# First attention: four tasks of its software pipeline change their slots, and the square of q and k moves behind an exponential

## The reference

```python
qkv = x @ Wqkv.T + bqkv                    # x: layer-normed, (16, 256, 128)
q, k, v = (qkv[:, :, 0], qkv[:, :, 1], qkv[:, :, 2])   # 16 heads of 8 channels
q = rms_norm(q, qn_w)                      # q / sqrt(mean(q*q) + 1e-6) * w, for each head
k = rms_norm(k, kn_w)
scores = jnp.einsum('bhsd,bhtd->bhst', q, k) * scale
attn = jax.nn.softmax(scores, axis=-1)
out = jnp.einsum('bhst,bhtd->bhsd', attn, v)
return out.reshape(B, S, D) @ Wproj.T + bproj          # added to x
```

## Time and profile before

| | before |
|---|---|
| median of 3 runs | 1019.81 us (1018.68 to 1025.88) |
| the profiled execution | 1023.82 us, span 1022.0 us |
| mean granted clock of TensorE | 0.965 |
| busy: PE / PEld / DVE / ACT / POOL | 86% / 61% / 71% / 57% / 51% |
| exponentials of attention a (L414) | 128, 1024 ns each, 33.1 us idle in front of them |
| values of attention a (L315) | 1024 matmuls, 72.0 us busy |

### The profile page before, as it was taken

The page is one execution under the profiler, slowest core; times in us unless marked ns, Lnnn a source line. Parts: engine busy times, 40 slices in busy tenths (PEclk is TensorE's granted clock), DMA queues, the critical chain, the costliest instruction groups (busy, mean ns, idle before and its releaser), DMA issues.

```text
span 1022.0 us, 22245 instructions
## 1 busy us (share of the span) xinstructions
PE 883.0 (86%) x7264; PEld 625.6 (61%) x7264; DVE 728.8 (71%) x1970; ACT 579.1 (57%) x905; POOL 523.8 (51%) x606
## 2 busy tenths in 40 slices
PE   0589899987899999998788888888888789999998
PEld 0245555544588787886655555555554578878887
DVE  4357777766677777775657989898885477767765
ACT  1177777766544344443358888888886444344443
POOL 2556666656155545552425565666644364455441
PEclk9999999999799999998859999999997899999999
DMA  8000000000000000000000000000000000000000
GB/s 227 0 2 2 0 0 0 0 1 2 2 1 1 1 1 1 0 1 1 0 1 2 2 1 0 0 0 0 1 2 1 1 10 2 13 11 10 10 11 22
DMA packets 14591, 8.70 MB, mean 9 GB/s; under 512 B 1600, under 2 KB 14144, under 8 KB 14528
## 3 DMA queue, kind: packets, MB, share of 16 engines
q1 hardware_dynamic: 12944, 7.28, 2.5%
q10 hardware_dynamic: 1584, 0.62, 0.2%
HBM read 5.80 MB, written 2.10 MB: 8 GB/s over the span
## 4 chain that ended last, share of the span: by engine, by line
PE 21%; issue 13%; DVE 11%; POOL 7%; ACT 2%; DVEq 0%; POOLq 0%; ACTq 0%
DVE s_qs L1028 6%; PE psum L759 5%; PE psum L727 4%; POOL f_xe_lo L1374 3%; POOL f_p L1384 3%; PE psum L1267 2%; PE psum L709 2%; PE psum L1229 1%; PE psum L814 1%; DVE f_xe L1411 1%; PE psum L825 1%; PE psum L1231 1%; PE psum L1230 1%; PE psum L744 1%; ACT f_xe_hi L1343 1%
## 5 line engine op out<-in xcount | busy, mean ns | idle before, releaser
L1343 ACT ACTIVATE f_xe_hi<-f_xe 128x512 fp32r<-128x512 f32 x128 | 80.9, 632 | 202.8 <-DVE f_xe L1411 202.8
L1028 DVE TENSOR_REDUCE s_qs<-psum 128x4 fp32r<-128x1024 f32 x128 | 156.5, 1222 | 42.9 <-PE psum L744 42.2
L1374 POOL TENSOR_TENSOR f_xe_lo<-f_xe,f_xe_hi 128x512 fp32r<-128x512 f32 x64 | 83.7, 1308 | 192.7 <-ACT f_xe_hi L1343 192.7
L1267 PEld LDWEIGHTS psum<-w,f_h 128*128 128x128 f32 x1152 | 148.5, 192 | 8.8
L1267 PE MATMUL psum<-w,f_h 128*128 128x128 f32 x1152 | 153.8, 277 | 0.0
L414 ACT ACTIVATE s_probs<-psum 128x1024 f32<-128x1024 f32 x128 | 125.6, 1024 | 33.1 <-PE psum L301 32.9
L895 ACT ACTIVATE s_probs<-psum 128x1024 f32<-128x1024 f32 x128 | 131.2, 1025 | 19.2 <-PE psum L727 17.6
L1427 DVE TENSOR_TENSOR f_h<-psum,f_g 128x512 f32<-128x512 f32 x144 | 99.2, 689 | 49.2 <-ACT f_g L1328 33.9
L1229 PE MATMUL psum<-f_xe_hi,w_hi 128*128 128x512 f32 x288 | 127.6, 443 | 7.7 <-POOL f_xe_lo L1374 7.0
L1231 PE MATMUL psum<-f_xe_lo,w_hi 128*128 128x512 f32 x288 | 114.4, 397 | 0.0
L1230 PE MATMUL psum<-f_xe_hi,w_lo 128*128 128x512 f32 x288 | 113.8, 395 | 0.0
(11 more groups left out here) (179 smaller groups left out, 1757.1 us busy)
## 6 DMA issues: line engine op xcount, KB each, us to landing
x<-in_x SPq DMA_DIRECT2D x4, 512.0 KB, 9.5
out<-x SPq DMA_DIRECT2D x8, 256.0 KB, 2.3
w<-in_w SPq DMA_DIRECT2D x3, 512.0 KB, 6.7
select_raw<-in_select SPq DMA_DIRECT2D x1, 512.0 KB, 4.9
rope_cos<-in_rope_cos SPq DMA_DIRECT2D x1, 256.0 KB, 3.6
rope_sin<-in_rope_sin SPq DMA_DIRECT2D x1, 256.0 KB, 4.5
wqkv_a<-in_Wqkv_aT ACTq DMA_DIRECT2D x1, 192.0 KB, 6.0
bqkv<-in_bqkv ACTq DMA_DIRECT2D x1, 192.0 KB, 6.8
```

Source lines behind the costliest of these rows:

```text
L1028: dve.tensor_reduce(o[:, r:r + 2, 2 * p:2 * p + 2, 24:25].bitcast(F32R), M.rearrange("p (r j s) -> p r j s", r=2, j=2), AX.X, ALU.max, neg ...
L1267: ins = pe.matmul(Y[k % 2][:, t * P:(t + 1) * P], g.f_h[:, q, t * P:(t + 1) * P], g.w2[:, e, :], start=(e == 0 and t == 0), stop=(e == NE ...
L1374: pool.tensor_tensor(xe_lo[:, ring(e), :], src, xe_hi[:, ring(e), :], ALU.subtract).then_inc(xe_lo_pool.sem, 1)
```

## The change

Four tasks change their slots, and the key copy gets an entry of its own. In `AT_A`: normalise 8 to 10; x_turn 10 to 15; square, v copy 6 to 7; k_turn(1) 11 to 12; o_turn(1) 6 to 8, tokens(1) 7 to 8. The key copies stood in the slots of the k_turns, 7 and 11, and stand now in 7 and 13 (`kt_keep`). On ScalarE the code of the square moves ahead of that of the key copies, so that in slot 7 the order is exps(7), square, key copy.

```diff
--- before.py
+++ after.py
@@ -212,14 +212,15 @@
 
 
 STAGE_A = {"norm": 3, "xb": 2, "xt": 3, "qkv": 2, "square": 2, "sums": 2, "newton": 2, "rms": 2, "split": 1, "lo": 1,
-           "v": 1, "kt": 1, "qp": 1, "xt_keep": 3, "otr": -1, "atr": -1, "at_keep": -1, "pj": -1, "tokens": -1,
+           "v": 1, "kt": 1, "kt_keep": 1, "qp": 1, "xt_keep": 3, "otr": -1, "atr": -1, "at_keep": -1, "pj": -1, "tokens": -1,
            "residual": -1, "rstd": -1}
 
 
 AT_A = {
-    "pv": 5, "norm": (8,), "xb": (13,), "xt": (10,), "xt_keep": (15,), "qkv": (2, 4), "square": (6,), "sums": (7,),
-    "newton": (7,), "rms": (12,), "split": (2, 1), "lo": (3, 2), "v": (6,), "kt": (7, 11), "qp": (9, 14),
-    "otr": (3, 6), "tokens": (3, 7), "atr": (10,), "at_keep": (11,), "pj": (14,), "residual": (15,), "rstd": (15,),
+    "pv": 5, "norm": (10,), "xb": (13,), "xt": (15,), "xt_keep": (15,), "qkv": (2, 4), "square": (7,), "sums": (7,),
+    "newton": (7,), "rms": (12,), "split": (2, 1), "lo": (3, 2), "v": (7,), "kt": (7, 12), "kt_keep": (7, 13),
+    "qp": (9, 14), "otr": (3, 8), "tokens": (3, 8), "atr": (10,), "at_keep": (11,), "pj": (14,), "residual": (15,),
+    "rstd": (15,),
 }
 
 
@@ -416,8 +417,14 @@
             for h in part:
                 if att and h % EH == EH - 1:
                     exps(h)
-                for c in range(2):
-                    for off in due("kt", c, h, k):
+                for off in due("square", 0, h, k):
+                    m, km = n + off, k + off
+                    act.wait_ge(qkv_sb.sem, qkv_sb.upto(m))
+                    act.wait_ge(ss_sb.sem, ss_sb.upto(m - 1))
+                    act.activation(sq[:], qkv[:, km % 2, 0:2, :, :].rearrange("p a c d -> p (a c d)"),
+                                   ACT.Square).then_inc(sq_sb.sem, 1)
+                for c in range(2):
+                    for off in due("kt_keep", c, h, k):
                         m, km = n + off, k + off
                         act.wait_ge(kt_mm.sem, kt_mm.upto(m, c + 1))
                         act.activation(kt[:, km % 2, :, c * P:(c + 1) * P], four(QK),
@@ -427,12 +434,6 @@
                     act.wait_ge(xt_mm.sem, xt_mm.upto(m))
                     act.wait_ge(qkv_mm.sem, qkv_mm.upto(m - 1))
                     act.activation(xt[:], XB[:, 0:SEQ], ACT.Copy).then_inc(xt_sb.sem, 1)
-                for off in due("square", 0, h, k):
-                    m, km = n + off, k + off
-                    act.wait_ge(qkv_sb.sem, qkv_sb.upto(m))
-                    act.wait_ge(ss_sb.sem, ss_sb.upto(m - 1))
-                    act.activation(sq[:], qkv[:, km % 2, 0:2, :, :].rearrange("p a c d -> p (a c d)"),
-                                   ACT.Square).then_inc(sq_sb.sem, 1)
                 for off in due("at_keep", 0, h, k):
                     m, km = n + off, k + off
                     act.wait_ge(atr_mm.sem, atr_mm.upto(m))
```

## The result

The changed kernel took 1011.93 us in the median of 20 runs (1006.51 to 1017.49), the kernel before 1018.16 in the median of 20 (1015.06 to 1026.15). The ratio is 0.9929 with a 95% interval of 0.991 to 0.9949, so 7.2 us less (5.2 to 9.2). Forecast were 1009.4 us, a range of 1005.5 to 1017, and 0.54 for within 1%.

A forecast was written before the change was run, and what follows sets the result against it. No engine is full; each first-attention body is a ring of waits. Savings of 9.35 (bodies 1 to 11), 0.4 (body 0) and 0.7 (bodies 12 to 14) sum to 10.4 us off 1019.81: 1009.4 us, range 1005.5 to 1017.

The forecast's parts named there:

- The body: One sequence's pass through the first attention, bodies 1 to 11: shortened from 13.57 to 12.7 us.
- The tie of q_turn(1) with the second key copy: Late in the body, q_turn(1) and the key copy behind exps(13) fall together, at 11.0 and 10.96 us.
- The saving: Bodies 1 to 11 of the first attention: 0.85 us a body, bounds 0.6 and 1.0, together 9.35 us.
- The square: On ScalarE before exps(9): square and key copy need 1.12 us in a 0.7 hole, giving 0.75, not 1.03.
- Body 0 and bodies 12 to 14: First and late bodies of the first attention: gains of 0.4 us and, for the three late ones together, 0.7.
- The port: VectorE and GpSimd lock: addition moves from small copy to cast; about 0.15 us freed, up to 0.45 lost, a wash.
- The first rival: Bodies: collision lands wrongly or sums before tokens(1) hurt; up to 0.45 us a body lost, 1014.4 us; chance 0.21.
- Body 15 and 16 ...: 0: Bodies mixed with the feed-forward: o_turn(1) passes only scores(8) while TensorE is the slow one, so gain 0.
- The sum of 10.4: Whole kernel: 9.35 from bodies 1 to 11, 0.4 from body 0, 0.7 from bodies 12 to 14, in us.
- The forecast's last sentence: Forecast is wrong if the body exceeds 13.2 us or gains are given back at the feed-forward seam, after 255 us.
- Rival 2: Bodies: the ring has another, unseen part; gain under 0.2 us a body, about 1019 us; chance 0.08.
- rival 3: Second key copy behind exps(13) becomes the bound: q_turn(1) at 12.9, 0.95 us later, 1033 us; chance 0.08.

The follow-up runs named there:

- the second pair of traces: The kernel before and the changed kernel, each traced once more without edits: bodies 1 to 11 take 13.50 and 12.67 us each, spans 1014.3 and 1006.5 us.
- the undone moves: Changed kernel with square; x_turn, normalise; o_turn(1), tokens(1); or k_turn(1) and its copy put back, separately: bodies of 13.14, 13.24, 13.15, 12.89 us.
- the first three: Changed kernel with square; x_turn and normalise; or o_turn(1) and tokens(1) put back, separately: bodies lose 0.46, 0.56 and 0.47 us.
- the filled pair: The kernel before and the changed kernel, each with twelve idle transposes in TensorE's wait in body 15: medians 1015.87 and 1006.54 us.

## Why the prediction was right, point by point

**The body.** Laid out 12.7 us, measured 12.68 (12.50 and 12.83 in turn). Step by step in the slower body, forecast and measured: scores(8) 5.89 and 6.15; exps(9) 6.57 and 6.80; the first query copy 8.66 and 8.87; scores(12) 8.8 and 8.98; exps(13) 9.45 and 9.63; q_turn(1) 11.0 and 11.21; the next body 12.7 and 12.83. The first difference, 0.26 us, is in front of scores(8): project(1) waited for the eviction behind the held cast. In the faster body scores(8) came at 5.82. The tie of q_turn(1) with the second key copy was near but did not bind: the key copy L430 ends at 150.50 us, q_turn(1) starts at 150.57, which is the usual 1.01 us after values(2) (149.56).

**The saving was overstated.** I set the new body against one body of 13.57 us, the mean of bodies 1 to 11 was 13.46: 0.85 was 0.78, and 11 x 0.85 = 9.35 was 8.58 (9.03 by the second pair of traces).

**The square.** That it is not free was right, and that it alone gives nothing is shown. The prediction treated the moves as one layout; the undone moves show that each of the first three, taken back, loses more than half of the whole.

**Body 0 and bodies 12 to 14.** Body 0 gained 0.4 to 0.7 us, forecast 0.4, but only 0.2 in the filled pair; the same body 0 took 13.8 to 14.6 us in three traces after, so this term is not settled. Bodies 12 to 14 gained 1.98 by the two first traces, forecast 0.7. Without the low stretch, 1.5 us of it, about 0.5 is left: body 14's k_turn stayed GpSimd's, as said.

**The port.** "A wash" was near: the addition did reach the cast, 0.70 and about 0.5 us in turn instead of 0.41, and GpSimd still holds the small copy or the instruction in front of it. The first rival was the nearest of the rivals. It is 0.33 us in every other body here, 0.22 a body on the mean against the 12.46 with the addition moved, and it shows most, with a cast of 0.87 us, in the kernel with o_turn(1) taken back.

**The end.** What missed is "Body 15 and 16 ...: 0", with the silent premise behind it that all that follows takes as long as before. The sum of 10.4 was 9.4 to 10.2 at body 15 without low stretches (11.0 with the one in body 12), 9.9 to 10.8 in runs of equal granted clock, and 7.2 (5.2 to 9.2) in the measured times, because the changed kernel's mean clock was lower, 0.966 against 0.971. A low-clock stretch of 3.8 us at the seam to the mixture, in both traces after and one of two before, is the only difference of that size between body 15 and the end that the traces show beside the chance ones around attention b; that it makes up the whole of the lower clock is likely by the filled runs, and not shown. The forecast's last sentence named this place, without a price. That the time still fell near the middle of the range owes something to the range's width, which was made for scatter and for rival 1, not for the clock.

**Rival 2** (nothing moves) and **rival 3** (the key copy slower) fell: the key copy behind exps(13) ended at 11.1, not at 12.9, since exps(13) had come 1.7 us forward, and q_turn(1) did not wait for it.

## What to carry to other kernels

When several tasks of a hand-made pipeline stand between two events of its ring, lay the new order out as a whole with start-to-start distances from one profiled body: that came within 0.3 us at every step here, while single moves brought nothing or lost more than their share. Read the sum at the place where the edited part ends, not only in the total, and compare whole times at the same granted clock: here a third of the gain, 3 to 4 us, was hidden by the clock. After shortening a loop, look again at which GpSimd instruction now lies on which VectorE instruction.

## What the runs showed of the hardware

- VectorE can be held up for the length of a GpSimd instruction: the 128x512 cast L522 takes 0.41 us alone, 0.49 to 0.94 beside the 0.73 us addition, and 2.85 beside the 2.81 us low part of the weights; the 2-element copy L572 0.15 and 0.73; the v copy 0.28 and 2.46. GpSimd's own step L495 takes 0.90 us beside the casts in the slower body and 0.71 in the kernel with the addition moved. This agrees with the Trainium skill, "SBUF — State Buffer", section on SBUF's two separate sides. The evictions from PSUM beside the same GpSimd work (L579, 0.41 us; L606, 0.55) kept their length.
- One program, two executions: TensorE's granted clock at the seam was 0.72 in one and 1.00 in the other, 3.8 us apart at the end of the next layer. The summed low-clock time of the first four traces, in one-us windows, was about 72, 51, 58 and 58 us at times of 1023.8, 1016.1, 1008.9 and 1008.3 us.
- Twelve transposes without a use, 1.53 us of TensorE in a wait, stood in three traces, and the clock was at its upper level over the seam in all three; of the eleven traces without them, nine had a low stretch of 3.4 to 10.2 us there (of the ten that the expectation above speaks of, eight, not seven).
